# Householder steps on one core: three scalar products moved from VectorE to TensorE, and the order of two engines rewritten

## The reference, cut to what matters

```
deg = A.sum(0) + A.sum(1) - diag(A);  d = deg ** -0.5
L_norm = d[:, None] * (diag(deg) - A) * d[None, :]
_, U = eigh(L_norm)
agg = U.T @ features                # per batch
h   = relu(agg @ W1 + b1);  out = U @ (h @ W2 + b2)
```

## Time and profile before

| | |
|---|---|
| median of three executions | 4989.64 us |
| the profiled execution, its own time | 4989.5 us |
| its span, first to last instruction | 4987.7 us |
| DVE busy | 4026.5 us, 81% of the span |
| PE busy | 2551.1 us, 51% |
| ACT busy | 1139.3 us, 23% |
| steps with T = 4 (first root to first root of the next kind) | 55 to 859 us |
| steps with T = 3 | 859 to 1526 us |
| steps with T = 2 | 1526 to 2056 us |
| steps with T = 1 | 2056 to 2528 us |

### The profile page before, as it was taken

How to read it: one execution, slowest core, us unless ns; L and a number is a source line. 1 busy time by engine, 2 the same in 40 slices (tenths; PEclk the granted TensorE clock), 3 DMA queues, 4 the chain that set the end, 5 groups by cost and what they waited for, 6 DMA issues and landing times.

```text
span 4987.7 us, 116618 instructions
## 1 busy us (share of the span) xinstructions
PE 2551.1 (51%) x40168; PEld 1721.1 (35%) x40168; DVE 4026.5 (81%) x24921; ACT 1139.3 (23%) x5016; POOL 284.9 (6%) x1424
## 2 busy tenths in 40 slices
PE   4666666555556666544457645657423223135048
PEld 3444444444445555433322212322122223124024
DVE  7666666777777888888889999999967897988956
ACT  1212222222223333333311143333210200301001
POOL 1111111111110000000000000000000000000000
PEclk6555555555555555555567767778755555557579
DMA  2000000000000000000000000000000000000001
GB/s 69 2 2 2 2 2 2 2 2 2 2 2 3 4 4 4 3 3 2 3 1 1 1 1 1 1 1 1 1 1 0 0 0 0 0 0 1 0 0 34
DMA packets 20961, 20.11 MB, mean 4 GB/s; under 512 B 6544, under 2 KB 16784, under 8 KB 20368
## 3 DMA queue, kind: packets, MB, share of 16 engines
q1 hardware_dynamic: 20368, 12.65, 0.9%
HBM read 8.41 MB, written 4.20 MB: 3 GB/s over the span
## 4 chain that ended last, share of the span: by engine, by line
DVE 68%; PE 21%; issue 7%; ACT 2%; SPq 0%; DVEq 0%; DMA 0%; POOL 0%
PE bank L622 10%; DVE qp L1437 2%; DVE hid L1096 2%; DVE dif L1799 2%; PE bank L593 2%; PE bank L617 2%; DVE pcol L1076 2%; DVE tau_row L1084 2%; DVE qp L1424 2%; DVE gated L1082 2%; DVE ts L1040 1%; DVE yz L1055 1%; ACT ts L358 1%; DVE hid L1085 1%; PE bank L783 1%
## 5 line engine op out<-in xcount | busy, mean ns | idle before, releaser
L622 PE MATMUL bank<-lapw,hid 128*32 128x160 f32 (+3 forms) x10200 | 660.0, 420 | 81.5 <-DVE lapw L1105 58.3
L622 PEld LDWEIGHTS bank<-lapw,hid 128*32 128x32 f32 x10200 | 394.3, 162 | 200.0 <-DVE lapw L1105 79.7
L700 PE MATMUL bank<-hid,rows 128*128 128x512 f32 (+1 forms) x504 | 320.1, 802 | 275.3 <-ACT dif L410 271.9
L586 PE MATMUL bank<-xp,ones 128*32 128x1 f32 x4080 | 146.0, 202 | 458.1 <-DVE xp L1070 240.6
L371 ACT ACTIVATE swap<-vcols 128x4 f32<-128x4 f32 (+3 forms) x510 | 105.7, 207 | 1049.4 <-DVE xp L1070 696.8
L1050 DVE TENSOR_TENSOR yz<-bank,pick 128x128 f32<-128x128 f32 (+3 forms) x510 | 117.6, 231 | 233.7 <-PE bank L622 233.5
L700 PEld LDWEIGHTS bank<-hid,rows 128*128 128x128 f32 x504 | 118.7, 242 | 468.1 <-ACT dif L410 297.2
L586 PEld LDWEIGHTS bank<-xp,ones 128*32 128x32 f32 x4080 | 102.6, 140 | 501.4 <-DVE xp L1070 262.2
L593 PE MATMUL bank<-ycol,vcols 128*32 128x1 f32 x3064 | 89.8, 199 | 236.3 <-DVE ycol L1061 236.3
L593 PE MATMUL bank<-hid 128*32 128x1 f32 x3064 | 89.8, 199 | 191.6 <-DVE hid L1096 191.6
L586 PE MATMUL bank<-xn,ones 128*32 128x2 f32 x4080 | 141.2, 198 | 84.1 <-DVE xn L1009 84.1
(11 more groups left out here) (761 smaller groups left out, 8268.9 us busy)
## 6 DMA issues: line engine op xcount, KB each, us to landing
out_x<-xs SPq DMA_DIRECT2D x16, 256.0 KB, 2.5
lapw<-in_adj SPq DMA_DIRECT2D x1, 1024.0 KB, 5.3
bias_rows<-in_L_gnn_bg SPq DMA_DIRECT2D x8, 64.0 KB, 5.8
hid<-pair SPq DMA_DIRECT2D x32, 1.0 KB, 1.7
bias_rows<-in_L_gnn_b SPq DMA_DIRECT2D x4, 64.0 KB, 5.7
wg<-in_L_gnn_Wg SPq DMA_DIRECT2D x2, 64.0 KB, 4.8
wg<-in_L_gnn_W SPq DMA_DIRECT2D x2, 64.0 KB, 4.3
dif<-in_L_gnn_Wih SPq DMA_DIRECT2D x1, 0.5 KB, 7.1
```

The lines of the kernel that those rows point to most:

```text
L586: m = pe.matmul(into[32 * q:32 * q + 32, :], weights, column, start=True, stop=True)
L622: m = pe.matmul(bank[1][32 * q:32 * q + 32, 0:(T + 1) * 32].rearrange("p (u i) -> p u i", i=32), acols[:, t, k:k + 1].to_broadcast([P, 32] ...
L700: m = pe.matmul(bank[4 * h + q][:, 0:cols_], wih_t[:, p - 1, q * P:(q + 1) * P], hid[:, b0:b0 + nb, t:t + (nw - 1) * p + 1:p], start=True, ...
```

## The change

`dots(k)` goes; `product` makes norm, v*y and v*p for every T, and the root always has the small bias. A new predicate `gated_early(k)` (called `early`) is true for T = 3 and 4. There the tail is still summed on POOL, but PE broadcasts alpha and the tail between the groups of the strips, and DVE computes gate, `gated`, `tau_row`, `scrow` and `ats` ahead of the reductions that wait for `y_done`. For T = 1 DVE makes the products of the strips (`strips()`) ahead of `pair` and the panel products (`slots()`) between `pair` and `v`. For every T the reciprocal no longer waits for alpha, and L1040 no longer waits for the sign instruction.

```diff
-def dots(k):
-    return NT - (k + 1) // P <= DOT_TILES
+def gated_early(k):
+    return NT - (k + 1) // P >= 3
 # ACT
-                if dots(k):
-                    act.activation(ts[:, 7:8], tau_row[:, k:k + 1], ACT.Copy, scale=0.5)
+                act.activation(ts[:, 7:8], tau_row[:, k:k + 1], ACT.Copy, scale=0.5)
+                act.wait_ge(x2_ready, k + 1)
                 act.activation(w0[:, t0:], pcol[:, t0:], ACT.Copy, scale=tau_row[:, k:k + 1]).then_inc(w0_ready, 1)
 # PE
+                pe.wait_ge(a_ready, k + 1)
+                product(bank[0][:, 0:1], acols[:, t0:, k], acols[:, t0:, k]).then_inc(norm_ps, 1)
+                if not early:
                     everywhere(bank[5][:, 0:1], unit(k), acols[:, t0, k:k + 1]).then_inc(alpha_ps, 1)
-                else:
-                    pe.wait_ge(norm_in, 2 * (k + 1))
-                    everywhere(bank[0][:, 0:2], ones[:, 0:32], xn[:, 0:2]).then_inc(norm_ps, 1)
...
                     # after the group of tile t of the strips
+                    if t == t0 and early:
+                        everywhere(bank[5][:, 0:1], unit(k), acols[:, t0, k:k + 1]).then_inc(alpha_ps, 1)
+                    if t == t0 + 1 and early:
+                        pe.wait_ge(tail_in, k + 1)
+                        everywhere(bank[4][:, 0:1], ones[:, 0:32], xn[:, 2:3]).then_inc(tail_ps, 1)
...
-                    everywhere(bank[3][:, 0:1], ones[:, 0:32], xp[:, 0:1]).then_inc(vy_ps, 1)
-                    everywhere(bank[2][:, 4 * NB:4 * NB + 1], ones[:, 0:32], xp[:, 1:2]).then_inc(vp_ps, 1)
+                pe.wait_ge(x_ready, k + 1)
+                product(bank[3][:, 0:1], vcols[:, t0:, k], ycol[:, t0:]).then_inc(vy_ps, 1)
+                pe.wait_ge(x2_ready, k + 1)
+                product(bank[2][:, 4 * NB:4 * NB + 1], vcols[:, t0:, k], pcol[:, t0:]).then_inc(vp_ps, 1)
 # DVE, the new order of a step
+                dve.wait_ge(norm_root, k + 1)
+                a = put(V.reciprocal(ts[:, 3:4], ts[:, 0:1]))
+                if not early:
+                    dve.wait_ge(alpha_ps, k + 1)
+                    put(V.tensor_scalar(ts[:, 1:2], bank[5][:, 0:1], 0.0, 0.5, ALU.is_ge, ALU.subtract))
+                after(a)
+                a = put(V.tensor_scalar(ts[:, 4:5], ts[:, 3:4], bank[0][:, 0:1], ts[:, 0:1], ALU.mult, ALU.add))
+                if early:
+                    dve.wait_ge(alpha_ps, k + 1)
+                    a = put(V.tensor_scalar(ts[:, 1:2], bank[5][:, 0:1], 0.0, 0.5, ALU.is_ge, ALU.subtract))
+                if T == 1:
+                    z = strips()
+                after(a)
+                (pair twice; T == 1: slots(); v; inv)
+                if early:
+                    dve.wait_ge(tail_ps, k + 1)
+                    (gate, gated, tau_row with p_ready, scrow, ats)
+                if T > 1:
+                    z = strips()
+                    if j:
+                        c = slots()
+                after(z)
+                (ycol with x_ready; a1; not early: gate)
+                (pcol with x2_ready; not early: gated, tau_row; wait for x2_ready; bcol; not early: scrow; bm; not early: ats)
                 dve.wait_ge(vy_ps, k + 1)
                 V.scalar_tensor_tensor(acols[:, t0:, k + 1], ...).then_inc(a_ready, 1)
-                if k + 1 < STEPS and not dots(k + 1):
-                    norms(k + 1)
                 dve.wait_ge(vp_ps, k + 1)
                 dve.wait_ge(w0_ready, k + 1)
```

More of the change, by code:

```diff
@@ L356, in _ @@
                 act.wait_ge(norm_ps, k + 1)
[L357 to L360, removed]
+                act.activation(ts[:, 0:1], bank[0][:, 0:1], ACT.Sqrt, bias=tiny[:]).then_inc(norm_root, 1)
                 if k:
@@ L1031, in _, with strips @@
                     m.then_inc(updated, 1)
-                dve.wait_ge(norm_root, k + 1)
[L1034 to L1038, removed]
+                def strips():
+                    dve.wait_ge(y_done, k + 1)
+                    at = put(V.tensor_tensor(yz[:, t0:, 0:32], bank[1][:, 0:T * 32].rearrange("p (t i) -> p t i", i=32),
+                                             pick[:].unsqueeze(1).to_broadcast([P, T, 32]), ALU.mult))
+                    if j:
+                        dve.wait_ge(w2_ready, k)
+                        dve.wait_ge(v2_ready, k)
+                        at = put(V.tensor_tensor(yz[:, t0:, 32:32 + 2 * j], panel_cols(j, t0), panel_rows(bank[1][:, T * 32:T * 32 + 32], j, T), ALU.mult))
+                    return at
@@ L1044, in _ @@
+                if T == 1 and j:
+                    c = slots()
                 after(a)
-                vdone = put(V.scalar_tensor_tensor(v, onehot[:, t0:, k + 1], pair[:, k, 0:1], a_, ALU.mult, ALU.add))
+                put(V.scalar_tensor_tensor(v, onehot[:, t0:, k + 1], pair[:, k, 0:1], a_, ALU.mult, ALU.add))
                 after(b)
[L1047 to L1063, removed]
+                d = put(V.reciprocal(inv[:], pair[:, k, :]))
@@ L1064, in _ @@
+                if T > 1:
+                    z = strips()
+                    if j:
+                        c = slots()
+                after(z)
+                V.tensor_reduce(ycol[:, t0:], yz[:, t0:, 0:32 + 2 * j], AX.X, ALU.add).then_inc(x_ready, 1)
                 if j:
@@ L1067, in _ @@
                 a1done = put(V.tensor_reduce(a1[:, t0:], tz[:, t0:, 0:1 + 2 * j], AX.X, ALU.add))
[L1068 to L1072, removed]
+                if not early:
+                    dve.wait_ge(tail_ps, k + 1)
+                    g = put(V.tensor_scalar(gate_row[:, k:k + 1], bank[4][:, 0:1], 1e-24, -1.0, ALU.is_gt, ALU.mult))
                 after(a1done)
@@ L1075, in _ @@
                     dve.wait_ge(w0_ready, k)
[L1076 to L1084, removed]
+                V.scalar_tensor_tensor(pcol[:, t0:], a1[:, t0:], pair[:, k, 0:1], ycol[:, t0:], ALU.mult, ALU.add).then_inc(x2_ready, 1)
@@ L1085, in _ @@
+                if not early:
+                    after(max(d, g))
+                    g = put(V.tensor_scalar(gated[:], inv[:], gate_row[:, k:k + 1], None, ALU.mult))
+                    after(g)
+                    V.tensor_tensor(tau_row[:, k:k + 1], gated[:, 0:1], gated[:, 1:2], ALU.mult).then_inc(p_ready, 1)
+                dve.wait_ge(x2_ready, k + 1)
                 b = put(V.scalar_tensor_tensor(bcol_[:, t0:, k + 1], pcol[:, t0:], gated[:, 0:1], a1[:, t0:], ALU.mult, ALU.add))
-                dve.wait_ge(p_ready, k + 1)
@@ L1087, in _ @@
-                c = put(V.tensor_scalar(scrow[:, k:k + 1], tau_row[:, k:k + 1], gated[:, 0:1], -1.0, ALU.mult, ALU.mult))
+                if not early:
+                    dve.wait_ge(p_ready, k + 1)
+                    c = put(V.tensor_scalar(scrow[:, k:k + 1], tau_row[:, k:k + 1], gated[:, 0:1], -1.0, ALU.mult, ALU.mult))
                 after(b)
                 b = put(V.tensor_tensor(bm[:, t0:], bcol_[:, t0:, k + 1], ltm[:, t0:, k + 1], ALU.mult))
-                after(c)
-                c = put(V.scalar_tensor_tensor(ats[:, t0:], a_, scrow[:, k:k + 1], ltm[:, t0:, k + 1], ALU.mult, ALU.mult))
@@ L1092, in _ @@
-                if not dots(k):
-                    V.tensor_tensor_reduce(jcol[:, 2, t0:], v, pcol[:, t0:], 0.5, 0.0, ALU.mult, ALU.add, xp[:, 1:2]).then_inc(x2_ready, 1)
-                after(c)
+                if not early:
+                    after(c)
+                    b = put(V.scalar_tensor_tensor(ats[:, t0:], a_, scrow[:, k:k + 1], ltm[:, t0:, k + 1], ALU.mult, ALU.mult))
+                after(b)
                 dve.wait_ge(vy_ps, k + 1)
                 V.scalar_tensor_tensor(acols[:, t0:, k + 1], ats[:, t0:], bank[3][:, 0:1], bm[:, t0:], ALU.mult, ALU.add).then_inc(a_ready, 1)
-                dve.wait_ge(norm_ps, k + 1)
```

70 lines of the change are left out of this document (31 added, 39 removed).

## The result

The changed kernel takes 5119.66 us (median of 4, 5116.61 to 5120.62) against 4990.06 us (median of 4): a ratio of 1.0259, 95% interval 1.0241 to 1.0277. 4920 was forecast, with a range to 4975. The change makes the kernel slower by 130 us.

What follows compares the result with a forecast made beforehand. DVE and PE pass work to and fro, so their order in time bounds the kernel. Terms -42 (T = 4), +1 (T = 3), -6 (T = 2), -23 (T = 1) sum to -70 us from 4989.5: 4920, range 4875 to 4975.

Steps and rivals of the forecast that it cites:

- 0.12 for each tile: Products on PE: 0.12 us for each tile and 0.18 at the end, 0.66 for T = 4 and 0.54 for T = 3.
- the slack on DVE: T = 4, ahead of the strips' reductions: DVE free at 2.59 us, strips there at 2.69, so PE still decides.
- The first rival: Long runs of tiny matmuls don't keep the pace: 26 ns each, +111 us, time 5031; chance 9%.
- floor of about 25 ns: Rule against the forecast: v*y and v*p longer, about +81 us (T = 4) and +61 (T = 3), time some 5060.
- From Y to S on DVE: From DVE's first instruction needing the strips to the next strips' start: shorter by 0.59 us (T = 4), 0.82 (T = 3).
- From S to Y: From the strips' start on PE to DVE's first instruction needing them: longer by 0.26 us (T = 4), 0.83 (T = 3).
- the sum's +1 us: T = 3: -0.82 + 0.83 = +0.01 us a step in 128 steps, +1 us.
- T = 1: -28.1 for -23: T = 1: ycol starts 1.09 us after the reciprocal, not 1.27; -0.18 in 127 steps, -23 us.
- 57 instructions a microsecond with 51: PE's instruction rate after the change with T = 4, 57 per us, against 51 with T = 2; called near.
- The groups inside the strips: Two small matmul groups between the strips, 0.13 us each; rival at full 0.28: 4975, 11%; rival at nothing: 4897, 6%.
- y_done doesn't hold T = 1: Rival: T = 1 gains nothing because y_done holds pair or L1040's pitch is its full length; 4943, chance 10%.
- the prediction's fifth rival: TensorE's clock rises from 1.2 to 2.4 GHz and the strips halve: time 4856, chance 3%.

Runs made afterwards that it cites:

- the run with the order mended: Changed kernel with `product` running over tiles outside and quarters inside, also called the run with the loops swapped: 4960.12 us, ratio 0.9936.
- the best version: Changed kernel with gate behind the strips, products round the quarters, and for T = 3 and 4 the tail summed on POOL and broadcast: 4841.76 us, ratio 0.9701.
- the run with 16 more: Changed kernel with products round the quarters, and for T = 4 alpha's broadcast made twice, 320 PE instructions a step: 4974.57 us, ratio 0.9969.
- the late gate and the old order of the quarters: Changed kernel with gate, gated, tau, scale and ats behind the strips for every T, products still quarter by quarter: 5027.0 us, ratio 1.007.

## Why the prediction was wrong, step by step

**The step that failed: "0.12 for each tile", carried from a product of two tiles to products of three and four.** The pitch of 15 ns was a pitch of runs of 4 in a quarter of the array's columns. Matmul starts in the trace of the changed kernel, first to last of a product, come to 13.5 ns each with T = 1 and 15.0 with T = 2. With T = 3 and 4 the next product mixes in, so a whole product's turn is the measure: about 0.96 us for 32 with T = 4 (30 ns each), against 0.48. L1101 waits for v*y and v*p. In the step shown it starts 3.20 us behind L1017, not 2.04: 0.09 for v*y's later start, 0.45 for v*y's turn (0.93 for 0.48), 0.62 for v*p (1.35 for 0.73). The strips follow L1101 by 0.61 (0.62 reckoned). So the half behind L1017 grew by 1.15 over the forecast (3.81 for 2.66), and with T = 3 by 0.54 (2.82 for 2.28). That is (1.15 + 0.54) x 120 = 203 us on the steps without an update, if the few steps at the higher clock, told below, are left aside; the miss is 200 (5120 for 4920).

One reading beside it failed for the same reason. The result of v*y was to be at DVE at 1.56, before the next column's parts; the column (L1098) waits 0.70 us for it and starts at 2.31, not 1.61. The norm's product then starts at 2.81, not 1.89, and with T = 4 the root comes 0.64 us behind the strips' start and not 0.28. That used up the slack on DVE: in the step shown L1017 came at 2.74 with no idle time before it and 0.04 us behind the strips' end. That this half still came as forecast is partly luck.

The first rival named the sign and the place (v*y and v*p ahead of L1103), with a cause that the runs refute: not length but order. Its price of 26 ns was too low: it put that wait's end at 2.56 and the time at 5031, where 3.20 and 5120 were measured. (By its own sums it turns the change into a loss from about 23 ns on, not 22.)

The Trainium skill's floor of about 25 ns from start to start ("TensorE: Matmul & The Clock Gate", section "Wait — 56ns, not 53.3ns?") gave an estimate of 5060, closer than the forecast. As a floor it doesn't hold here: 32 matmuls going round the quarters come at 13.4 ns each. The same page's section "LDWEIGHTS (loading the stationary operand)" gives columns / 1.2 ns for a load, which makes an estimate of 26.7 ns for 32 columns. The trace agrees with that in part: in the norm product of T = 4 45% of the starts are 26 to 28 ns apart and 22% 53 to 54. No run here separates the load from the matmul, so that the weight loads of one quarter queue up is a reading, not shown; and it doesn't say by itself why most starts in runs of 4 are only 13 to 14 ns apart. Shown is that order and run length make the difference.

**Steps that held.** From Y to S on DVE: in the run with the order mended the half behind L1017 is 615.45 - 612.83 = 2.62 (forecast 2.66), and the step 5.27 (5.35). From S to Y: T = 4 2.74 (2.69), T = 3 2.43 (2.41). T = 3 without the fault is +0.02 a step (4.80 for 4.78; forecast +0.01), so the sum's +1 us for it was right (+2.1 measured). Behind it the early gate costs 61 us there, while the rest of the change, the products above all, gains 59 (608.1 against 667.3). T = 2: -7.0 for -6. T = 1: -28.1 for -23; L1061 stands where the sum put it, and the order's share was 20 for 16 reckoned (0.13 x 127).

**A cost not seen.** With the order mended the time is 4960 and not 4920, and PE stands still for 46 us with T = 4, which no term of the sum allows for. The prediction compared 57 instructions a microsecond with 51 and called the pair near. Nowhere in the steps of before does PE stand for "issue". The rate doesn't explain it: the best version has 304 instructions in 5.37 us, 57 a microsecond, and doesn't stand.

**Rivals.** The groups inside the strips cost a little less than the 0.13 taken: 0.11 for a further one (the run with 16 more), and with two of them L1017 stands 2.65 us behind the strips' start in the run with the order mended, 2.43 before. y_done doesn't hold T = 1. The clock rose after all, seldom: see below. It is no part of the gain from the swapped loops, for it favours the changed kernel: 0.53 on average with T = 4, against 0.50 in the run with the loops swapped.

## What to carry to other kernels

A price per instruction, read from a short run, belongs to the run's order as well as its size: before more of them are put in a row, look at which part of the array each takes. For scalar products by broadcast columns, as here, let the tiles be the outer loop and the four quarters the inner: 160 us of 5120 in this kernel. Moving work ahead of a wait pays only up to the idle time in front of that wait; beyond it, it belongs behind, where it fills gaps.

## What the runs showed of the hardware that was not expected

**The clock rises for single stretches.** In the changed kernel 14 steps of T = 4 take 5.2 to 5.6 us among neighbours of 6.5. Three windows, one ahead of such a step, one over it and one over the next (columns: length, then busy time of PE, PEld, DVE, ACT, POOL, then the granted clock):

```profile
76.00:80.00 4.00, 3.16 (x104) 3.10 (x97) 2.44 (x13) 0.82 (x5) 0.83 (x5) 0.50 0.01 2
80.69:86.20 5.51, 4.65 (x168) 4.49 (x164) 4.17 (x24) 1.37 (x10) 0.94 (x5) 0.81 0.03 6
86.20:92.50 6.30, 5.42 (x159) 5.05 (x155) 3.96 (x23) 1.14 (x8) 1.01 (x6) 0.50 0.01 3
```

For most of the fast step the clock was 2.4 GHz, not 1.2, with PE busy 79% in the four microseconds before. The mean over T = 4 is 0.53, and the kernel before has 0.50 in all its steps. A busier PE alone didn't bring it: with the late gate and the old order of the quarters PE was busy 98% of the time with T = 4, and the clock stayed at 1.2 GHz. The premise of the prediction's fifth rival, that sustained activity releases the clock, isn't borne out by this run:

```profile
55.00:951.00 896.00, 878.34 (x22513) 836.42 (x22514) 498.97 (x2950) 179.39 (x1034) 25.80 (x127) 0.50 0.02 4
```

**Weights of 128 columns** take eight instructions 1.87 us; the same product as 32 instructions of 32 columns round the quarters takes 0.61.
